# Causal mask inside the scores' contraction, keys in strips of 64, a fourth block of probabilities added on GpSimd, and two buffers for the later blocks

## What is computed

```python
q = einsum('bld,dhk->blhk', x, Wq)
latent = einsum('bld,dc->blc', x, Wkv_down)              # 32 channels
k, v = (einsum('blc,chk->blhk', latent, W) for W in (Wk_up, Wv_up))
attn = softmax(where(causal, einsum('bqhd,bkhd->bhqk', q, k) / 8, -max))
y = einsum('bqhd,hdo->bqo', einsum('bhqk,bkhd->bqhd', attn, v), Wout)
# ffn(x) = x @ int4(kernel) + bias + (x @ a) @ b
x = x + 0.5 * ffn(layernorm(x)); x = x + attention(layernorm(x)); x = x + 0.5 * ffn(layernorm(x))
```

## Time and profile before

| what | value |
|---|---|
| device time, median of 3 runs | 907.95 us (906.62 to 909.5) |
| profiled execution | 905.89 us, of which its span is 904.2 us |
| granted clock of TensorE, mean | 0.983 |
| busy PE, PEld | 844.8 us, 579.0 us |
| busy POOL, DVE, ACT | 732.9 us, 659.2 us, 550.1 us |
| DMA | 77.9 MB in 77547 packets, mean 86 GB/s |

### The profile page before, as it was taken

The page is one execution under the profiler, slowest core; times in us unless marked ns, Lnnn a source line. Parts: engine busy times, 40 slices in busy tenths (PEclk is TensorE's granted clock), DMA queues, the critical chain, the costliest instruction groups (busy, mean ns, idle before and its releaser), DMA issues. The chain is left out here.

```text
span 904.2 us, 21710 instructions
## 1 busy us (share of the span) xinstructions
PE 844.8 (93%) x7766; PEld 579.0 (64%) x7766; DVE 659.2 (73%) x1840; ACT 550.1 (61%) x1113; POOL 732.9 (81%) x834
## 2 busy tenths in 40 slices
PE   6688999999999999999999999999999999999886
PEld 4455666666576766667576766667676666757455
DVE  3597677678778677778868768877867767776645
ACT  4435666757666565757766665756766675656551
POOL 4304889998989989898998989898998999889732
PEclk9878999999999999999999999999999999999999
DMA  4445241524435151533535151443525152330000
GB/s 102 117 116 137 56 115 45 120 75 96 115 83 128 41 132 39 127 84 84 127 72 139 34 128 50 108 104 84 127 63 132 31 127 59 91 96 15 13 25 13
DMA packets 77547, 77.90 MB, mean 86 GB/s; under 512 B 9392, under 2 KB 51136, under 8 KB 77440
## 3 DMA queue, kind: packets, MB, share of 16 engines
q1 hardware_dynamic: 76640, 75.45, 34.5%
q10 hardware_dynamic: 800, 1.07, 0.4%
HBM read 9.90 MB, written 8.39 MB: 20 GB/s over the span
## 5 line engine op out<-in xcount | busy, mean ns | idle before, releaser
L491 POOL TENSOR_TENSOR first_probs<-first_probs,later_probs 128x768 f32<-128x768 f32 x240 | 371.4, 1556 | 23.0 <-PE bank L765 23.0
L601 ACT ACTIVATE later_probs<-bank 128x384 f32<-128x384 f32 (+1 forms) x448 | 231.0, 539 | 154.5 <-PE bank L752 154.2
L1088 DVE TENSOR_REDUCE maxima<-bank 128x1 f32<-128x512 f32 (+1 forms) x384 | 255.1, 682 | 62.0 <-PE bank L821 61.8
L752 PE MATMUL bank<-q_stack,keys 123*128 123x512 f32 (+1 forms) x704 | 280.5, 424 | 9.8 <-ACT first_probs L601 8.3
L821 PE MATMUL bank<-keys,q_stack 122*128 122x512 f32 (+3 forms) x1024 | 254.6, 337 | 10.1 <-DVE maxima L1088 2.5
L821 PEld LDWEIGHTS bank<-keys,q_stack 122*128 122x128 f32 x1024 | 181.3, 193 | 86.6 <-DVE block_max L1088 26.6
L601 ACT ACTIVATE first_probs<-bank 128x512 f32<-128x512 f32 x256 | 139.8, 594 | 98.8 <-PE bank L752 94.0
L1088 DVE TENSOR_REDUCE block_max<-bank 128x4 f32<-128x512 f32 x256 | 173.9, 679 | 32.8 <-PE bank L821 32.1
L752 PEld LDWEIGHTS bank<-q_stack,keys 123*128 123x128 f32 x704 | 127.9, 191 | 57.9 <-ACT first_probs L601 30.1
L524 POOL TENSOR_SCALAR_AFFINE_SELECT later_probs<-later_probs 128x512 f32<-128x512 f32 x192 | 124.0, 646 | 46.3 <-ACT later_probs L601 46.1
L765 PE MATMUL bank<-later_probs,lat 128*32 128x384 f32 (+2 forms) x1536 | 109.7, 388 | 0.7 <-POOL later_probs L524 0.7
(11 more groups left out here) (143 smaller groups left out, 898.6 us busy)
## 6 DMA issues: line engine op xcount, KB each, us to landing
q_stack<-q_high SPq DMA_DIRECT2D x256, 128.0 KB, 2.4
q_stack<-q_low SPq DMA_DIRECT2D x128, 128.0 KB, 2.5
out_dram<-x SPq DMA_DIRECT2D x32, 256.0 KB, 2.9
x_in<-in_L_attn_x_bld_dram SPq DMA_DIRECT2D x16, 256.0 KB, 3.3
x_back<-out_dram SPq DMA_DIRECT2D x16, 256.0 KB, 2.9
keys<-keys_staged SPq DMA_DIRECT2D x15, 192.0 KB, 2.5
keys<-keys_staged SPq DMA_DIRECT2D x30, 96.0 KB, 2.3
lat<-lat_staged SPq DMA_DIRECT2D x16, 64.0 KB, 1.9
```

What stands on the lines that cost most here:

```text
L491: nc.gpsimd.tensor_tensor(total, total, later_probs[j - 1][:, heads], ALU.add).then_inc(added, 1)
L601: nc.scalar.activation(probs_of(s)[:, e:e + heads, 0:n], score_bank(t, u)[:, 0:heads * n].rearrange("p (e q) -> p e q", e=heads), ACT.Exp) ...
L752: nc.tensor.matmul(score_bank(t, u)[:, 0:heads * n], keys[par][:, PLAIN_BLOCK[j], :], q_stack[par][:, first:first + heads, j * P:L], start ...
L1088: nc.vector.tensor_reduce(out, seg, AX.X, ALU.max).then_inc(a_free, 1)
```

## The change

The tile of the causal mask goes from 128 queries by 128 keys to 64 by 64. Keys are stored in 34 strips of 64, some of them twice, with mask rows (22 instead of 26) or without; queries are stored by pairs of heads (`g` even and odd), eight tiles of 64 queries each. Two heads' 64 queries make the 128 partitions of a maxima matmul, which then needs 64 to 512 keys in steps of 64. The scores of a block's own 128 queries (part `None` in `BANKS`) are made with the mask rows, as two matmuls of 4x64 columns for four heads into one bank; the later queries (the other parts) are made without. The `affine_select` on GpSimd is gone; block 3 is now added on GpSimd as well, and `weigh_ones` runs once a group. The later blocks have two buffers each. All tables count in scores (44 a round) instead of steps, on each engine by itself, and a position of 44 or more lies in the next round. Keys take five DMAs instead of three. Weights that are used only at the start now share buffers with later tiles. In the last round the adds, block 3's among them, are DVE's.

```diff
-HALF_UNITS = ([unit for h in (0, 4, 2, 6) for unit in (
-    [(h, 3)], [(h, 2), (h, 0)], [(h + 1, 3)], [(h + 1, 2), (h + 1, 0)], [(h, 1), (h + 1, 1)])])
+HALF_UNITS = ([unit for p in (0, 2) for unit in (
+    [(p, 7)], [(p, 6), (p, 0)], [(p, 5), (p, 1)], [(p, 4), (p, 2)],
+    [(p + 1, 7)], [(p + 1, 6), (p + 1, 0)], [(p + 1, 5), (p + 1, 1)], [(p + 1, 4), (p + 1, 2)], [(p, 3), (p + 1, 3)])])
...
+PARTS_OF = [[None, (0, 1), (1, 1), (2, 1), (3, 1)], [None, (0, 2), (2, 2)], [None, (0, 4)], [None]]
+BANKS = [(g, j, part) for g in range(G) for j, parts in enumerate(PARTS_OF) for part in parts]
...
+WEIGH_AT = [[5, 8, 14, 14], [21, 21, 21, 21], [31, 34, 34, 34], [40, 47, 47, 47]]
+ONES_AT = [19, 31, 40, 52]
...
-ADDED = [1, 2]
-DEN_PARTS = [3, 0]
+ADDED = [1, 2, 3]
...
-        q_stack = [sb(f"q_stack{i}", [KM, H, L], F32R) for i in range(2)]
-        keys = [sb(f"keys{i}", [KM, KEY_BLOCKS, P], F32R) for i in range(2)]
+        q_stack = [sb(f"q_stack{i}", [KM, H // 2, SUB, 2, HALF_TILE], F32R) for i in range(2)]
+        keys = [sb(f"keys{i}", [KM, STRIPS, HALF_TILE], F32R) for i in range(2)]
...
-        later_probs = [sb(f"later_probs{j}", [P, HG, L - P * j]) for j in range(1, TT)]
+        later_probs = [[sb(f"later_probs{j}_{i}", [P, HG, L - P * j]) for j in range(1, TT)] for i in range(2)]
...
                 def add_probs(off, g, j, part):
...
-                    wait_batch(pool, p_ready, t, off, STEPS, g * TT + j + 1)
+                    wait_batch(pool, exp_done, t, off, SCORES, scores_by(g * TT + j))
...
-                        diag = probs_of(s)[:, :, 0:n]
-                        nc.gpsimd.affine_select(out=diag, in_=diag, compare_op=ALU.is_ge, fill=0.0, base=0,
-                                                pattern=[[0, HG], [1, n]], channel_multiplier=-1).then_inc(p_ready, 1)
...
+                def exp(u):
...
+                    if part is None and j == 0:
+                        wait_batch(act, den_done, t, 0, G, g - 1)
+                    elif part is None:
+                        wait_batch(act, pv_done, t, 0, STEPS, (g - 2) * TT + j + 1)
+                        wait_batch(act, added, t, 0, G * GROUP_ADDS, (g - 2) * GROUP_ADDS + PARTS * j)
...
+                def score(u):
...
-                    nc.tensor.matmul(score_bank(t, u)[:, 0:heads * n], keys[par][:, PLAIN_BLOCK[j], :],
-                                     q_stack[par][:, first:first + heads, j * P:L], start=True, stop=True).then_inc(s_full, 1)
...
+                    if part is None:
+                        for half in range(2):
+                            w = 2 * j + half
+                            out = bank[:].rearrange("p (e q) -> p e q", e=HG)[:, :, half * HALF_TILE:(half + 1) * HALF_TILE]
+                            last = nc.tensor.matmul(out, strips(par, KM, OWN[w]), q_stack[par][:, pair:pair + HG, w, of, :],
+                                                    start=True, stop=True)
+                    else:
+                        e, heads = part
+                        last = nc.tensor.matmul(bank[:, 0:heads * (n - P)], strips(par, KM, LATER[j]),
+                                                q_stack[par][:, pair + e:pair + e + heads, 2 * (j + 1):SUB, of, :],
+                                                start=True, stop=True)
...
-                    wait_batch(pe, p_ready, t, off, STEPS, s + 1)
...
+                    wait_batch(pe, exp_done, t, off, SCORES, scores_by(g * TT + j))
...
-                def weigh_ones(off, s):
...
+                def weigh_ones(off, g):
...
+                    wait_batch(pe, added, t, off, G * GROUP_ADDS, (g + 1) * GROUP_ADDS)
+                    for i in range(TT):
...
+                    for p, w in unit:
+                        n = HALF_TILE * (w + 1)
+                        queries = q_stack[(par + off) % 2][0:KC, half * PAIRS + p, w].rearrange("r e q -> r (e q)")
+                        last = nc.tensor.matmul(bank[:, col:col + n], queries, strips((par + off) % 2, KC, SEEN[w]),
+                                                start=True, stop=True)
...
+                        strip = P if w == 5 else HALF_TILE
+                        out = strip_max[:, half, 6 - w, p, 0:L // strip]
...
+                        for of, first, end in ((0, 0, 7), (1, 0, 3), (2, 0, 5), (2, 5, 8)):
+                            w = (6, 5, 4)[of] if first == 0 else 2
+                            nc.vector.tensor_reduce(maxima[:, half, :, w], strip_max[:, half, of, :, first:end], AX.X, ALU.max)
+                        nc.vector.tensor_copy(maxima[:, half, :, 0], strip_max[:, half, 0, :, 7])
+                        nc.vector.tensor_copy(maxima[:, half, :, 1], strip_max[:, half, 1, :, 3]).then_inc(max_made, 1)
```

More of the change, by code:

```diff
@@ L1080, in max_unit @@
                         return
[L1081 to L1088 removed]
+                    p, w = unit[0]
@@ L1155, in closing @@
                     moments(t_stats, t_mv, t_dve, 1, 1, -1, t_moments)
[L1157 to L1159 removed]
+                for u in range(SCORES):
+                    if prep and u == SUM_AT:
                         wait_batch(dve, f_full, t, 2, F_UNITS, 2)
```

739 lines of the change are left out of this document (342 added, 397 removed).

## The result

The changed kernel takes 812.85 us (median of 4 runs, 812.19 to 813.53) against 908.04 us: a ratio of 0.895, 95% interval 0.894 to 0.897. The forecast was 854 us with a range of 835 to 890. The direction was right, the size was not: the gain is 95 us where 54 were forecast, and the range begins 22 us above the result. All times are medians of executions in the fast state; one of the four of the last experiment's kernel ran in a slow one (1316.7 us, mean granted clock 0.81) and is left out.

The account below looks back on a forecast made before the run. Two nearly full engines, PE and POOL, passing work to each other were taken as the bound. Rounds of 44.5 + 3.5 = 48.0 us save 15 x 3.4 = 51, start and end 3: 852 us profiled, 854 forecast, range 835 to 890.

Parts of the forecast that it names:

- POOL's, DVE's and ACT's times: Busy times in a round: POOL from 46.6 to 42.5 us, DVE from 39.4 to 38.5, ACT unchanged at 33.3.
- the price of the 256 add: Adds of 256 elements a partition on POOL, eight more a round: 0.75 us each, 5.8 us together less overlap.
- score pieces of 64 at no price: Score matmuls on PE streaming 64-column pieces and writing them apart into PSUM: no extra cost; other bound twice the columns' time.
- "slower" rival: Score matmuls reading pieces of 64 queries take twice the time: 9.5 us more, rounds of 57.5 us, 996 us; chance 0.09.
- "POOL stays the bound": 256 adds cost 1.29 us each, rounds of 51.9 us, about 912 us; chance 0.06 together with dearer writes.
- PE's work: Summed PE work in a round: 46.1 us before, 44.5 us after, 1.6 us less.
- "12 stretches in column tiles x 0.2": PE's way into and out of column tiles: 2.4 us a round; nine stretches instead of twelve save 0.6 us.
- the stall: PE standing still in a round: 5.3 us before, taken as 3.5 us after.
- Start and end: Outside the 15 rounds: 2 us less from four fewer maxima, 1 us from fewer ones and no masks; together 3.
- "the stall nearly goes": PE's stall nearly vanishes: rounds of 46 us, 824 us; chance 0.10 for below 837 us.

Follow-up runs that it names:

- the last experiment's kernel: The changed kernel with each own block's scores as one matmul of 512 columns instead of two of 4x64, without causal mask: 812.4 us, ratio 0.894.

## Why the prediction was wrong

**Right.** The direction; POOL's, DVE's and ACT's times; the price of the 256 add; score pieces of 64 at no price (812.4 us with 16 matmuls a round fewer, 812.9 with them). So the "slower" rival was void, and so was "POOL stays the bound". Against the price of nothing stood a rule of the Trainium skill ("TensorE: Matmul & The Clock Gate", Part 3, The mechanism) that weight loads overlap running matmuls only when they go to other row groups, though the same section also lets a load into a background buffer go ahead. By the rule it would have been an estimated 1.7 us a round; these two times disagree with it.

**Wrong, PE's work, a term that was mis-sized.** "12 stretches in column tiles x 0.2": a stretch costs 0.33 us, so three fewer save 1.0 us, not 0.6. PE's work was 47.4 us, not 46.1, so 1.3 of the 5.3 us that the prediction called stall were work. It fell by 2.25 us where 1.6 were forecast, 0.65 us a round, 10 us of the 41 between forecast and result. The stretches are 0.4 of the 0.65. The rest is within the sum itself: its own terms (0.6, 0.9 and 0.6 less, 0.1 to 0.3 more) add up to 1.8 to 2.0 less, and 1.6 was taken.

**Wrong, the stall, the step that failed.** "PE's stall is bounded by 0 and today's 5.3 us. I take 3.5: the waits for the mask and for single buffers go, those for DVE and ACT stay". By the ledger it went from 4.0 to 0.65 us. The masks gave 0.02 us a round by themselves, and 0.8 once maxima were moved as well; single buffers put back into the new order cost a steady round nothing. The waits for DVE and ACT, which were to stay, are nearly all that went, and a lighter DVE or ACT was not enough for it: with the changed kernel's DVE and ACT work and the old places of the maxima the stall is 6.3 us. What I did not weigh was the part of the change that has no duration: tables of places on every engine, counted in scores instead of steps. I priced instructions and asked which resource was lighter. The kernel before was held by loops through PE, DVE, ACT and POOL in fixed orders, and none of these engines was full.

What is shown: with all of the change's lighter work but the old places of the maxima, rounds are 51.4 us; with the old order and masks and four sets of ones gone, 50.9. So lighter work and POOL's relief show little or nothing in a round without the order. The stall's 3.35 us over 15 rounds are 50 us, the work's 2.25 are 34. What isn't shown is how much of the order's gain each table holds, nor whether this order could be had without the rest of the change: with masks on POOL the one version that I tried was far slower, so the mask's removal may have been needed to let POOL's order be as it is, though its time was not.

**Start and end.** Forecast 3 us, measured 8.9 outside the 15 rounds, of which 5.2 are the second buffers in the final round, where I had expected 1 us from fewer ones and no masks.

The rival "the stall nearly goes" (824 us) was the nearest and got 0.10. Its counter-argument, POOL at 42.5 and DVE at 38.5 of 46 us "each in a fixed order", is the error in short: fixed orders can be fitted, and these were.

## What to carry to other kernels

In a pipeline of engines with fixed orders, a busy share near 90% need not be a bound (POOL's 91% of a round was none), and a stall has no price of its own: work in a round plus stall is the round, and a stall removed at one place returned at another until the second loop was cut too. Before costing a change, follow the chain back from a stalled instruction until it repeats one round earlier, find a second chain of like length, and only then ask what the change does to both. Count which instructions really stand in the chain: 4 of 8 spreads left out did, and they gave 0.85 us where 1.2 to 1.7 were expected. When the diff changes tables of places, give the range room down to PE's bare work: here one table was worth 83 us with the same instructions, in the company of the other new tables.

## Not expected of the hardware

- Entering and leaving 32-column tiles costs 0.14 and 0.20 us on PE (by the ends of matmuls in the changed kernel), not symmetric, and not seen in busy times, since matmuls' records overlap.
- In the kernel with masks in the new order, where PE stood for 18 of 75.1 us a round, the granted clock of the round was 0.84 on average between its levels of 1.2 and 2.4 GHz (window 371.3 to 446.4 us). Each of its five falls to 1.2 GHz stands within, or less than 1.1 us behind, a stretch of 2.0 to 5.4 us in which PE ran nothing. PE is busy for 56.8 us of that round against 46.6 in the kernel with the ones of block 3 apart, which has the same matmuls, so long stalls cost a second time there. The kernels with rounds of 45.8 to 53 us kept 1.00 in their steady rounds, but for one fall of 3.4 us in the kernel with moved maxima:

```profile
371.30:446.40 75.10, 56.77 (x494) 43.43 (x495) 38.30 (x117) 33.96 (x69) 46.49 (x50) 0.84 0.28 67
```
